# Cross-attention with an image branch: two of ten score tiles, instead of one, turned on TensorE, and two, instead of three, left to VectorE's second product

## The reference

```
q = heads(hidden_states @ W_q);  k_t, v_t = heads(text_ehs @ W_k), heads(text_ehs @ W_v)
probs_t  = softmax(q k_t^T * attn_scale)                 # 8 x 20 x 512 x 508
text_out = probs_t v_t
qsem     = l2norm(probs_t text_ehs)                      # over 512 columns
sem      = qsem l2norm(ip_ehs)^T                         # 4 image tokens
probs_ip = softmax(q k_ip^T * attn_scale + 0.5 * sem) * spatial_mask
out      = (text_out + probs_ip v_ip) @ W_out + b_out + hidden_states
```

## Time and profile before

| | |
|---|---|
| median of 3 executions | 1608.22 us (1607.81 to 1612.23) |
| profiled execution | 1612.23 us, its span 1610.5 us |
| TensorE matmuls | 1541.2 us, 96% of the span |
| VectorE | 1303.4 us, 81% |
| GpSimd | 1248.7 us, 78% |
| ScalarE | 1027.5 us, 64% |
| mean granted clock of TensorE | 0.985 |

### The profile page before, as it was taken

The page is one execution under the profiler, slowest core; times in us unless marked ns, Lnnn a source line. Parts: engine busy times, 40 slices in busy tenths (PEclk is TensorE's granted clock), DMA queues, the critical chain, the costliest instruction groups (busy, mean ns, idle before and its releaser), DMA issues.

```text
span 1610.5 us, 38783 instructions
## 1 busy us (share of the span) xinstructions
PE 1541.2 (96%) x13066; PEld 920.6 (57%) x13066; DVE 1303.4 (81%) x3245; ACT 1027.5 (64%) x2289; POOL 1248.7 (78%) x1187
## 2 busy tenths in 40 slices
PE   4999999899999999999999999999999999999996
PEld 2777667555555555555555555555555555555553
DVE  6455554688997978997899789978988899789976
ACT  4455655666766666766676667666766676667751
POOL 4233233789898888998898889888988899889982
PEclk9899999899999999999999999999999999999998
DMA  5455767888899998999899989998999799989984
GB/s 207 133 165 145 201 178 187 165 140 138 162 140 186 165 176 141 195 164 170 147 183 166 179 147 186 165 175 152 178 163 181 145 182 177 177 144 169 165 139 98
DMA packets 723627, 264.66 MB, mean 164 GB/s; under 512 B 686665, under 2 KB 712914, under 8 KB 723442
## 3 DMA queue, kind: packets, MB, share of 16 engines
q1 hardware_dynamic: 722242, 260.53, 86.8%
q10 hardware_dynamic: 1200, 1.80, 0.3%
HBM read 68.51 MB, written 34.55 MB: 64 GB/s over the span
## 4 chain that ended last, share of the span: by engine, by line
PE 66%; DVE 11%; POOL 8%; issue 6%; DMA 5%; ACT 3%; SPq 1%; DVEq 0%; ACTq 0%
PE bank L1636 22%; PE bank L1637 14%; PE bank L1689 13%; PE bank L1593 6%; DMA late<-spare 4%; DVE probs L1250 3%; DVE neg_max L1238 3%; POOL probs L752 3%; PE bank L1641 2%; POOL wkv L745 2%; PE bank L1635 2%; POOL spare L745 2%; PE bank L1666 2%; PE bank L1750 2%; ACT probs L864 1%
## 5 line engine op out<-in xcount | busy, mean ns | idle before, releaser
L1636 PE MATMUL bank<-u_sb,late 127*128 127x508 f16 x2560 | 946.8, 376 | 0.0
L1637 PE MATMUL bank<-u_sb,late 127*128 127x508 f16 (+3 forms) x2560 | 763.5, 298 | 0.0
L1238 DVE TENSOR_REDUCE neg_max<-bank 128x1 f32<-128x508 f32 x640 | 434.7, 679 | 156.8 <-PE bank L1593 154.8
L1635 PE MATMUL bank<-v_ring,late 127*128 127x42 f16 x2560 | 468.3, 183 | 20.3 <-DMA late<-spare 11.2
L745 POOL TENSOR_TENSOR wkv<-probs,wkv 128x508 f16<-128x508 f32 x360 | 405.4, 1132 | 89.0 <-ACT wkv L876 87.2
L1250 DVE SCALAR_TENSOR_TENSOR probs<-bank,probs 128x508 f32<-128x508 f32 x640 | 431.9, 675 | 5.9 <-PE bank L1637 5.9
L1635 PEld LDWEIGHTS bank<-v_ring,late 127*128 127x128 f16 x2560 | 246.8, 96 | 255.8 <-DMA late<-spare 14.3
L864 ACT ACTIVATE probs<-bank,exp_bias 128x508 f32<-128x508 f32 x576 | 383.7, 666 | 0.1
L853 ACT ACTIVATE exp_bias<-neg_max 128x1 f32<-128x1 f32 x576 | 116.7, 203 | 390.5 <-DVE neg_max L1238 389.4
L1636 PEld LDWEIGHTS bank<-u_sb,late 127*128 127x128 f16 x2560 | 248.1, 97 | 192.0 <-issue 2.5
L745 POOL TENSOR_TENSOR spare<-probs,spare 128x508 f16<-128x508 f32 x216 | 247.6, 1149 | 58.7 <-ACT spare L876 56.2
(11 more groups left out here) (194 smaller groups left out, 1682.1 us busy)
## 6 DMA issues: line engine op xcount, KB each, us to landing
raw<-k_parts SPq DMA_DIRECT2D x192, 79.4 KB, 3.8
raw<-in_ctx_cols SPq DMA_DIRECT2D x8, 1016.0 KB, 7.3
raw<-q_parts SPq DMA_DIRECT2D x32, 240.0 KB, 3.7
v_parts<-v_sb SPq DMA_DIRECT2D x8, 840.0 KB, 11.8
v_ring<-v_parts SPq DMA_DIRECT2D x32, 210.0 KB, 4.3
u_parts<-u_sb SPq DMA_DIRECT2D x8, 825.5 KB, 8.8
u_sb<-u_parts SPq DMA_DIRECT2D x8, 825.5 KB, 5.6
raw<-in_x_cols SPq DMA_DIRECT2D x8, 768.0 KB, 4.4
```

Of the source, the lines that this page charges most:

```text
L1238: nc.vector.tensor_reduce(neg_max[:, v % 4:v % 4 + 1], bank[s_bank(v)][:, 0:T], AX.X, ALU.max, negate=True)\
L1635: nc.tensor.matmul(o, hi_k, v_ring[0:TP, n, h, k, :], start=(k == 0), stop=False)
L1636: nc.tensor.matmul(y, hi_k, u_sb[0:TP, par, GH[k]:GH[k] + T], start=(k == 0), stop=False)
L1637: done = nc.tensor.matmul(y[:, k * TP:T], hi_k, u_sb[0:TP, par, UL[k]:UL[k] + U_COLS[k]], start=False, stop=(k == TT - 1))
```

## The change

Two rows of constants, and all that follows from them:

```
-    PERIOD, PLAIN_AT = 10, (0,)
+    PERIOD, PLAIN_AT = 10, (0, 5)
     TURNED = [v for v in range(UNITS) if v % PERIOD not in PLAIN_AT]
-    SECOND_AT = (3, 6, 9)
+    SECOND_AT = (4, 9)
```

## The result

The changed kernel takes 1622.58 us (median of 4, 1620.85 to 1627.76) against 1608.51 us (median of 4, 1607.81 to 1612.23): ratio 1.009, 95% interval 1.0072 to 1.0108. It is slower, beyond the 0.3% that can be told. The forecast was 1614 us with a range of 1600 to 1631, so the time lies in the range, but 8.6 us above the point. Its profiled execution took 1616.23 us (span 1614.3), 4.6 us less than the fastest of the four.

What follows compares the result with a forecast made beforehand. TensorE was taken as the bound, its feeders sometimes late. 28.8 - 8.4 - 3.4 - 9.5 - 1.0 - 1.5 + 0.5 = +5.5 us on the profile; with 0.5 us more, 6 us on the median: 1614 us, range 1600 to 1631.

Steps and rivals of the forecast that it cites:

- TensorE's price: Four transposes in each of 64 more units lengthen TensorE's pace by 0.45 us per unit: +28.8 us.
- The feeders' work: GpSimd and VectorE swap operations of like length, ScalarE's small addition is hidden, one DMA transpose of nine goes: nothing added.
- The waits for a DMA: TensorE's 16 waits for DMA transposes, 20.2 us, shrink as the slower TensorE lets feeders catch up: -9.5 us.
- The waits for the exponential: TensorE's 24 waits for the exponential, 9.9 us, each shrink by up to 0.45 us: -8.4 us.
- The restart: Each TensorE wait that goes saves 0.16 us beyond its idle time: -3.4 us for exponential waits, -1.0 for DMA.
- The clock, -1.5 us: Half-speed clock stretches behind long TensorE waits partly vanish: -1.5 us, between 0 and -4.5.
- The base: The profiled execution before lay 4.0 us above the median; having less to win back ordinarily adds 0.5 us to the rise.
- The sum against the profile: All terms together against the profiled execution of 1612.23 us: +5.5 us, so 1617.7 us.
- The late weighing: Rival: at j of 25 VectorE's norm waits for GpSimd's `weigh_plain`, up to 8 us instead of 0.5: 1621.5 us; chance 0.12.
- Waits stay: Rival: TensorE itself sets the feeders' lead, so no wait shrinks: 1637 us, or 1647 us; chance 0.12.
- all waits go: Rival: fewer DMA transposes shorten the landing too, so all TensorE waits are paid back: -10.7 us, 1597.5 us; chance 0.12.
- the clock: Rival: transposes do not hold TensorE's clock up, so plain units bring low-clock stretches: 96 us more, 1710 us; chance 0.02.

Runs made afterwards that it cites:

- the run with one piece: Changed kernel, but in the 64 added plain units only the first of four pieces is transposed; 1602.67 us, ratio 0.9948.
- added transposes alone: Kernel before plus four unread fp32 transposes of a constant tile on TensorE in each of 64 units, all else unchanged; 1625.0 us, ratio 1.0083.
- the first pair of profiles: First profiled executions of the kernel before and the changed kernel: 1612.23 and 1616.23 us.
- the loads spread: Kernel before, with a group's ten loads issued in parts between units instead of one piece behind the tenth; 1599.78 us, ratio 0.9935.
- the second pair: Both kernels run and profiled once more, source unchanged: before 1609.22 us, changed 1624.65 us; units take 1283.0 and 1295.1 us in the profiles.
- the kernel with plains alone: Kernel before with two plain units of ten but still three second units, so GpSimd weighs five of ten; 1610.9 us, ratio 1.0001.

## Why the prediction was right in sign and short in size

- **TensorE's price, +28.8 us: right.** 2.26 us against 1.82 in the units with transposes. With one transpose instead of four, in the run with one piece, it is 1.93 us: 0.11 us each. The added transposes alone leave a rise of 14 us after the feeders have had their gift.
- **The feeders' work, nothing: right by sum.** GpSimd and VectorE moved by under 10 us over the whole span. What the prediction did not see is that the zero on GpSimd is made of two halves of different worth: minus one weighing with the plain unit, plus one with the second unit. Alone, they gave 0 and +31 us, up to 12 of it the clock.
- **The waits for a DMA, -9.5 us: the mechanism right, the size within its bounds.** They fell by 13.3 us in the first pair of profiles, more than forecast, and by 3.9 in the second, 12.0 to 8.1. How that divides between TensorE's slowness and the DMA's relief stays open: with the added transposes alone the waits are 10.7 us, which leaves 9.5 and 3.8 us for the two by the first profiles, 1.3 and 2.6 by the second.
- **The waits for the exponential, -8.4 us: wrong.** They were to fall under 2 us and are 7.3. The step "each shrinks by up to 0.45 us" failed at two places. One is the wait at 422 us, which grew by 0.97 us. The other is near j of 31, where VectorE is late by 0.65 us in 6 batches, with 0.16 us of restart each: 4.9 us. VectorE's step of the batch before takes 1.51 us there. It took as much in six of seven batches of the kernel before, and in some of them the wait for a DMA (1.23 us at 848.21) will have hidden the one for VectorE: with the loads spread it comes out in two of the batches (0.74 and 0.64 us). That is not all: the batch from some 620 to 780 us had no wait for a DMA there. It had these two short ones, where the changed kernel has one long one (before, then after):

```profile
689.40 0.38 PE L1593 MATMUL bank<-raw 96*128 96x508 bf16 x1 [0.17 <-ACT probs L864]
...
691.62 0.39 PE L1593 MATMUL bank<-raw 96*128 96x508 bf16 x1 [0.26 <-ACT probs L864]
```

```profile
684.33 0.37 PE L1593 MATMUL bank<-raw 96*128 96x508 bf16 x1 [0.67 <-ACT probs L864]
```

So the first of them has grown with the change, and the second is gone. Why it grew stays open. In the second pair the waits for the exponential did fall by 5.5 us, since the second profile of the kernel before had more of them, 12.8 us.

- **The restart, 0.16 us a wait: right in size.** In the units of the changed kernel with a wait, the distance from scores to scores is longer than pace and idle time together by 0.15 to 0.18 us (18 units). The waits over 0.06 us went from 45 to 18 in the first pair and from 41 to 15 in the second, 26 x 0.16 = 4.2 us, which I had at 4.4.
- **The clock, -1.5 us: too small.** At the lower clock the units lost 9.9 us between the first profiles (15.5 to 5.6) and 6.8 between the second, so 5.0 and 3.4 us by the half that the prediction used.
- **The base: the mis-sized term.** I noted that the profiled execution of before lay 4.0 us above the median and put 0.5 us on the rise for it. Most of the 8.6 us by which the forecast is short had to be there. With the second pair the books close: 28.8 - 3.9 - 5.5 - 4.2 - 3.4 (half of 6.8 us less at the low clock) = 11.8 us against 12.1 measured in the units. They close with the first pair too: 28.8 - 13.3 - 2.6 - 4.3 - 5.0 = 3.6 against 4.3. What I called savings of 23.3 us is 15 to 17 in ordinary executions.
- **The sum against the profile, +5.5 us: met by luck.** The two first profiles differ by 4.0 us. But that of the changed kernel is, by the clock, near its fastest, 6.4 us under its median, and within the sum the exponential's waits gave 5.8 us less than forecast while the DMA's waits and the clock gave 3.8 and 3.5 more.
- **The late weighing: refuted.** The weighing of the unit in question starts at 832.81 us and takes 1.15; the norm that needs it starts at 834.67, 0.71 us after its end, and as much in every other batch but the first (2.4 us). I had put the new operation where an old one stood, without asking whether GpSimd would still be as late there. The new waits after j of 30 that this rival foretold did come, without any wait for GpSimd's weighing.

```profile
832.81 1.15 POOL L759 TENSOR_TENSOR probs<-probs,spare 128x508 f32<-128x508 f32 x1
```

```profile
834.67 0.68 DVE L1250 SCALAR_TENSOR_TENSOR probs<-bank,probs 128x508 f32<-128x508 f32 x1
```

- **Waits stay, all waits go, the clock: all three out.** The clock over the units reads 1.00 with twice the transposes. The median time to landing of a unit's transpose is 3.3 us in both kernels, so the usual landing did not become shorter; of the late ones, over 4.5 us, there are 71 of 507 in the units instead of 119 of 571.

Left open: why the unprofiled executions of the changed kernel sit mostly at a clock of 0.983 to 0.985, no higher than those of the kernel before, while both its profiled ones had more (0.989 and 0.986) and few low stretches in the units. The table by clock works around it and does not explain it.

## What to carry to other kernels

When work is moved on to the engine that sets the pace, its feeders get the same time as a gift; count their waits as money that may pay for it, but count them over several executions, not in the one that was profiled. A wait that is named after a DMA can belong to whoever feeds the DMA, or to what stands before it in the queue: vary the feeder's operations by one for ten units, and the queue's order, and see which the wait follows. Where a change has two parts, cost each alone, since a zero sum can be a gain and a loss. And before a fixed place is credited with a wait that goes, look at all engines there in the kernel with the change: a step can take longer in its new company.

## What the runs showed of the hardware

Four fp32 transposes of 128 x 128 take 0.45 us of TensorE's pace, 0.11 us each, though each record is 274 ns long. A wait of TensorE costs some 0.16 us more than its idle time in the records.

Between executions of one program the mean granted clock differed by up to 0.008 (0.981 to 0.989, 71 executions of the kernel before), and 0.001 less went with some 1.5 us more there and 1.7 us more in the changed kernel.

The issue of a group's ten loads in one piece kept the next unit's transpose back by 4.8 to 6.8 us from the first load's issue; spread over nine units the loads cost some 11 us less.

One step of VectorE with two inputs (L1417) took 0.68 us in all seven batches of the kernel with plains alone, where it began in a pause of GpSimd, and 1.51 us in all seven of the changed kernel, where GpSimd ran back to back. That GpSimd is the reason is not shown by a run of its own.
